# A four-layer cross-attention kernel on one core: the gelu of layer 2 as a tanh of a polynomial, for three batches in four

## What is computed

```
out = attn(layer_norm(q), layer_norm(kv))            # layer 2, 16 heads of 16
out = q + jax.nn.gelu(ctx @ Wo + bo, approximate=False)
...
x = residual + _mha(x, base_n, W_qkv, b_qkv, W_o, b_o)     # layer 3, 8 heads of 32
U = (xn @ W_in.T + b_in) @ Bmat
def step(s, u_t):
    s = jax.nn.silu(s @ A.T) + u_t
    return (s, s)
```

## Time and profile before

| | us |
|---|---|
| median of 3 runs | 1515.5 |
| the runs | 1513.93 to 1517.46 |
| profiled execution, its time | 1517.49 |
| profiled execution, its span | 1515.9 |
| PE busy, share | 1346.9, 89% |
| ACT busy, share | 1065.2, 70% |
| DVE busy, share | 1039.8, 69% |
| POOL busy, share | 82.9, 5% |

### The profile page before, as it was taken

One profiled execution on the slowest core, in us unless ns is written; L12 is line 12 of the kernel. 1 busy time (PEld: TensorE's weight loads), 2 busy tenths in 40 slices (PEclk: granted clock), 3 DMA queues, 4 the chain that ended last, 5 costly groups with the idle time before them and its releaser, 6 DMA issues.

```text
span 1515.9 us, 35932 instructions
## 1 busy us (share of the span) xinstructions
PE 1346.9 (89%) x13436; PEld 1002.6 (66%) x13436; DVE 1039.8 (69%) x2323; ACT 1065.2 (70%) x3212; POOL 82.9 (5%) x145
## 2 busy tenths in 40 slices
PE   7999899988998889999888999988899999788855
PEld 6788666665675556777666677766676777566644
DVE  4676757756787778687777777877776787777400
ACT  4556677757788887777787677777866777787422
POOL 2000111110000000000000000000000000000000
PEclk9999999999999999999999999999999999999855
DMA  8222310012221122121101211201121121110100
GB/s 296 85 87 98 103 56 2 1 46 95 58 85 42 44 75 68 42 71 57 57 30 57 83 31 58 85 29 54 47 70 43 43 85 57 29 50 9 43 0 14
DMA packets 69883, 90.42 MB, mean 60 GB/s; under 512 B 5520, under 2 KB 58896, under 8 KB 69328
## 3 DMA queue, kind: packets, MB, share of 16 engines
q1 hardware_dynamic: 69600, 87.87, 18.2%
q0 software_dynamic: 112, 0.26, 0.1%
HBM read 71.33 MB, written 16.78 MB: 58 GB/s over the span
## 4 chain that ended last, share of the span: by engine, by line
PE 60%; DVE 14%; ACT 14%; issue 10%; POOL 0%; DMA 0%; ACTq 0%; DVEq 0%; SPq 0%; POOLq 0%
PE ps L1320 14%; PE ps L1694 11%; PE ps L1327 8%; PE ps L1334 7%; PE ps L1723 6%; ACT arena L790 5%; DVE arena L1269 5%; PE ps L1768 3%; PE ps L1397 2%; PE ps L1521 2%; PE ps L1538 2%; PE ps L1677 2%; DVE arena L949 2%; ACT R L850 1%; DVE nmax L1252 1%
## 5 line engine op out<-in xcount | busy, mean ns | idle before, releaser
L1320 PE MATMUL ps<-W,arena 128*128 128x128 f32 x2896 | 434.6, 284 | 22.3 <-ACT arena L790 19.8
L1320 PEld LDWEIGHTS ps<-W,arena 128*128 128x128 f32 x2896 | 324.9, 145 | 171.5 <-issue 129.5
L790 ACT ACTIVATE arena<-ps,nmax 128x512 f32<-128x512 f32 x640 | 435.1, 686 | 0.2
L797 ACT COPY arena<-ps 128x512 f32<-128x512 f32 x320 | 187.3, 585 | 213.0 <-PE ps L1320 208.9
L1249 DVE TENSOR_REDUCE nmax<-ps 128x1 f32<-128x512 f32 x320 | 206.1, 686 | 119.5 <-PE ps L1694 83.3
L1269 DVE COPY arena<-ps 128x512 f32<-128x512 f32 x320 | 213.8, 686 | 23.7 <-PE ps L1320 13.5
L1694 PE MATMUL ps<-W,arena 32*128 32x512 f32 x1280 | 185.2, 646 | 35.3 <-DVE arena L1269 34.2
L1723 PE MATMUL ps<-arena 128*32 128x128 f32 x5120 | 173.4, 276 | 31.6 <-ACT arena L797 31.4
L1252 DVE TENSOR_REDUCE nmax<-ps 128x2 f32<-128x1024 f32 x160 | 193.7, 1210 | 0.0
L1723 PEld LDWEIGHTS ps<-arena 128*32 128x32 f32 x5120 | 130.4, 110 | 69.5 <-ACT arena L797 59.1
L790 ACT ACTIVATION_READ_ACCUMULATOR arena<-ps,nmax 128x1 f32 x640 | 131.1, 205 | 0.0
(11 more groups left out here) (240 smaller groups left out, 1648.0 us busy)
## 6 DMA issues: line engine op xcount, KB each, us to landing
W<-keys SPq DMA_DIRECT2D x48, 512.0 KB, 3.7
arena<-values SPq DMA_DIRECT2D x48, 512.0 KB, 5.1
keys<-W SPq DMA_DIRECT2D x16, 448.0 KB, 3.0
values<-W SPq DMA_DIRECT2D x16, 448.0 KB, 3.6
W<-keys SPq DMA_DIRECT2D x16, 256.0 KB, 2.8
arena<-values SPq DMA_DIRECT2D x16, 256.0 KB, 3.3
W<-in_pack SPq DMA_DIRECT2D x1, 3180.0 KB, 10.5
CX<-in_ctx SPq DMA_DIRECT2D x4, 512.0 KB, 11.0
```

What stands on the lines that cost most here:

```text
L790: nc.scalar.activation(Pr[:, a, :], ps[:, a, :], ACT.Exp, bias=nmax[:, u % 32:u % 32 + 1], accum_out=den[:, u % 32:u % 32 + 1]).then_inc(s ...
L797: nc.scalar.copy(PT[:, (4 * Q + a) % 8, :, :].rearrange("p k n -> p (k n)"), psT).then_inc(sem("u_ev_act"), 1)
L1320: ins = nc.tensor.transpose(dst[:, k * P:(k + 1) * P], src[:, k * P:(k + 1) * P], ident)
```

## The change

For the batches 0 to 2 the gelu is computed as 0.5 x (1 + tanh(p(x))). POOL computes p(x): it clamps x to +-5.7, squares it, and evaluates a polynomial of seven coefficients in the square by multiply and add in turn, then multiplies by x. That is 14 instructions of 128 x 256 values in float32, each behind a wait for the one before. ScalarE takes the tanh of the result in place (L793 in the new numbering), and VectorE puts the rest together in two instructions (L1262 and L1264) in place of one add. The new tiles `bent` lie in the part of `W` that held `inw`, which is not used any more by then. The batch 3 keeps its gelu and its steps. In the chains of the batches 0 to 2 gelu, statistics, norm and transpose move four steps back, from 4, 5, 6, 6 to 8, 9, 10, 10, and what hangs on the transpose with them; POOL's part stands at step 3. Calls of `after_steps` get the batch as a second argument.

```diff
@@ -132,11 +134,18 @@
-def after_steps(li):
+ERF_AT = 5.7
+ERF_TANH = (0.7978849414816304, 0.03633308446488688, -3.2594837808075025e-05, -5.5306259012116404e-05,
+            3.964757753935919e-06, -1.322645093331823e-07, 1.7562063102252576e-09)
+ERF_OPS = 2 * len(ERF_TANH)
+def after_steps(li, b):
-                 2: dict(gelu=4, stats=5, nrm=6, tp=6), 3: dict(bias=2, stats=3, nrm=4, tp=4)}[li])
+                 2: dict(gelu=8, stats=9, nrm=10, tp=10) if b < 3 else dict(gelu=4, stats=5, nrm=6, tp=6), 3: dict(bias=2, stats=3, nrm=4, tp=4)}[li])
...
@@ -305,6 +314,8 @@
+        spare = Carve(W[:, PLAN["inw"][0]:PLAN["outw"][0]])
+        bent = [[spare.take(D) for _ in range(3)] for _ in range(2)]
...
@@ -499,12 +510,36 @@
             pool.memset(UT[:, (NCH - 1) * P + 1:NCH * P, NB - 1], 0.0)
             pool.memset(UT[:, 0, :], 0.0).then_inc(sem("zeroed"), 1)
 
+            def bend(c, b):
+
+                x, x2, r = bent[b % 2]
+                n = 3 * c + b
+                done = itertools.count(ERF_OPS * n + 1)
+                if n:
+                    pool.wait_ge(sem("L2_gelu"), c * NB + b + 1 - 1)
+                pool.wait_ge(sem("L2_pre"), c * NB + b + 1)
+                nc.gpsimd.tensor_scalar(x, orows[b % 2], ERF_AT, -ERF_AT, ALU.min, ALU.max).then_inc(sem("L2_bent"), 1)
+                pool.wait_ge(sem("L2_bent"), next(done))
+                nc.gpsimd.tensor_tensor(x2, x, x, ALU.mult).then_inc(sem("L2_bent"), 1)
+                pool.wait_ge(sem("L2_bent"), next(done))
+                nc.gpsimd.tensor_scalar(r, x2, ERF_TANH[-1], ERF_TANH[-2], ALU.mult, ALU.add).then_inc(sem("L2_bent"), 1)
+                for a in ERF_TANH[-3::-1]:
+                    pool.wait_ge(sem("L2_bent"), next(done))
+                    nc.gpsimd.tensor_tensor(r, r, x2, ALU.mult).then_inc(sem("L2_bent"), 1)
+                    pool.wait_ge(sem("L2_bent"), next(done))
+                    nc.gpsimd.tensor_scalar(r, r, a, None, ALU.add).then_inc(sem("L2_bent"), 1)
+                pool.wait_ge(sem("L2_bent"), next(done))
+                nc.gpsimd.tensor_tensor(r, r, x, ALU.mult).then_inc(sem("L2_bent"), 1)
+
             def chain_of(o, b):
                 G, wq = OCTETS[o]
                 c, li, _ = STAGES[G]
                 if LAYERS[li].quads != 2 * (wq + 1):
                     return
-                n, step = turn_side(G), after_steps(li)
+                n, step = turn_side(G), after_steps(li, b)
+                if li == 2 and b < 3:
+                    yield step["add"]
+                    bend(c, b)
                 if li:
                     yield step["stats"]
                     norm({1: "L2", 2: "L3", 3: "u"}[li], n, b % 2)
...
@@ -753,8 +788,12 @@
-                    act.wait_ge(sem("L2_pre"), n)
-                    nc.scalar.activation(nrm[i], orows[i], ACT.Gelu).then_inc(sem("L2_gelu"), 1)
+                    if b < 3:
+                        act.wait_ge(sem("L2_bent"), ERF_OPS * (3 * c + b + 1))
+                        nc.scalar.activation(bent[i][2], bent[i][2], ACT.Tanh).then_inc(sem("L2_gelu"), 1)
+                    else:
+                        act.wait_ge(sem("L2_pre"), n)
+                        nc.scalar.activation(nrm[i], orows[i], ACT.Gelu).then_inc(sem("L2_gelu"), 1)
...
@@ -1218,7 +1257,14 @@
-                    add_more(row, row, nrm[i])
+                    if b < 3:
+                        own["sums"] += 2
+                        nc.vector.scalar_tensor_tensor(orows[i], bent[i][2], 1.0, orows[i], ALU.add, ALU.mult).then_inc(sem("row_sum"), 1)
+                        dve.wait_ge(sem("row_sum"), own["sums"] - 1)
+                        nc.vector.scalar_tensor_tensor(row, orows[i], 0.5, row, ALU.mult, ALU.add).then_inc(sem("row_sum"), 1)
+                        dve.wait_ge(sem("row_sum"), own["sums"])
+                    else:
+                        add_more(row, row, nrm[i])
```

More of the change, by code:

```diff
@@ L741, in chain_of @@
                 c, li, _ = STAGES[G]
-                l, i, n, step = LAYERS[li], b % 2, turn_side(G), after_steps(li)
+                l, i, n, step = LAYERS[li], b % 2, turn_side(G), after_steps(li, b)
                 if l.quads != 2 * (wq + 1):
```

1 line of the change is left out of this document (added).

## The result

| | before | after |
|---|---|---|
| median, us (20 executions each) | 1515.27 | 1519.78 |
| the executions, us | 1511.69 to 1518.57 | 1513.73 to 1527.24 |
| ratio, 95% interval | | 1.0031 [1.0016, 1.0046] |
| profiled execution, its time, us | 1517.49 | 1515.4 |
| its span, us, and granted clock | 1515.9, 0.961 | 1513.8, 0.961 |

The forecast was 1512.3. The median moved the other way, by +4.5 us, while the two profiled executions, which had the same granted clock of TensorE, differ by 2.1 us in the direction of the forecast. That contradiction is what the experiments are about.

The account below looks back on a forecast made before the run. The prediction took a loop run once per quad of four heads, across several engines, as the bound. Chunk 0 +0.6, chunks 1 to 3 -6.2 and the collision +2.4 gave -3.2 us: 1515.5 to 1512.3, range 1496 to 1521.

Parts of the forecast that it names:

- The bounding views: What bounds the kernel: no engine is full; the loop each quad of four heads runs once, TensorE 60% of chain.
- part 1: Third quad of a stage loses two table loads and the gelu: -1.38 us in chunk 0, -2.27 later.
- Part 2: Norm, transpose, query projection and evictions go from a stage's fourth quad (-0.71, -0.86 us) to the next stage's second (+0.93, +1.08).
- Part 3: VectorE's add and statistics, now ahead of the copies in the next stage's first quad, delay the following scores: +1.36 us.
- Part 4: Third batch's query evictions meet the fourth batch's gelu on ScalarE: 0.6 us once per chunk, +2.4 in all.
- Part 5: POOL's polynomial, 7.5 to 10.7 us, is covered by two whole quads and about 2 us more: costs nothing.
- The sum: Chunk 0 +0.6 us, chunks 1 to 3 -6.2, the collision +2.4: together -3.2 us.
- The step from the sum to the median: The -3.2 us summed from the profiled execution is applied to the median of 1515.5, giving 1512.3 us.
- D is worse than its parts: Rival: work queued in the next stage's second quad adds 0.4 us per batch, +4.8, so 1517 us; chance 0.17.

## Why the prediction was wrong

**The bounding views and part 1 (loads and gelu leave A): right.** A is 5.54 in chunk 0 and 5.86 later, forecast 5.55 and 5.86. ScalarE lost 30.1 us, forecast 30.8.

**Part 2 (projection from B to D): right in chunk 0, half in the others.** B is 5.55 in chunk 0, forecast 5.54. In the scan chunks it is 6.05, 5.99 and 5.67 for the three batches, forecast 5.63 for all. I had read one batch's B in before and used it for nine, and that very batch, the second, came out at 5.99: -0.50, forecast -0.86. The tail was misread. In chunk 0 I took it from C, in chunk 1 from 785.99 to 788.18, which is D and has 2.19 us. C's own, in before, starts here and ends at the scores of 782.23, 2.42 us:

```profile
779.81 0.66 PE L1320 MATMUL ps<-W,arena 128*128 128x128 f32 x4
```

In after that B's tail is 2.55:

```profile
773.65 0.65 PE L1366 MATMUL ps<-W,arena 128*128 128x128 f32 x4
...
776.20 1.14 PE L1740 MATMUL ps<-W,arena 32*128 32x512 f32 x8 [0.32 <-DVE arena L1315]
```

D was spared a part of what B kept: it is 6.81, 6.83 and 6.79, and for the second batch +0.88, forecast +1.08 (7.03). In chunk 0 it is 6.55, forecast 6.59.

**Part 3 (VectorE's block in C): right.** +1.38 in chunk 0, forecast +1.36; 7.13 to 7.14 later, forecast 7.22. The releaser of D's scores is L1315, as forecast, and C ahead of it was not free. The run with the block one step later shows the same from the other side: C falls by 1.37.

**Part 4 (the collision): right in kind, the term too small.** Two rows of before in chunk 3, the copy of ScalarE that starts A' and the values that wait for the second one:

```profile
1368.69 0.59 ACT L797 COPY arena<-ps 128x512 f32<-128x512 f32 x1
...
1371.60 1.08 PE L1723 MATMUL ps<-arena 128*32 128x128 f32 x32 [0.61 <-ACT arena L797]
```

and the same place of after:

```profile
1363.32 1.16 PE L1373 MATMUL ps<-arena,W 128*128 128x128 f32 x8
...
1364.95 0.59 ACT L836 COPY arena<-ps 128x512 f32<-128x512 f32 x1 [0.35 <-PE ps L1366]
...
1365.50 0.61 ACT L761 ACTIVATE arena<-ps,bq 128x128 f32<-128x128 f32 x2
...
1368.36 1.08 PE L1769 MATMUL ps<-arena 128*32 128x128 f32 x32 [1.55 <-ACT arena L836]
```

The scores of A' start at 1369.14 in before and at 1364.96 in after. Before, ScalarE's copy was 0.45 us ahead of them, now it is level. Its row says that it waited 0.35 us for a transpose of TensorE. Two things that part 2 moved stand ahead of it in D now, the query projection on TensorE (L1373) and the evictions of the norm on ScalarE (L748); no run separates them there. So from scores to values it is 3.40 in place of 2.46: +0.94. The evictions are 0.5 of it, as two runs show (8.76 against 8.25 where they alone are added, 8.68 against 9.18 where they alone are taken away), a little under the 0.6 that I counted, and 0.4 is the lost lead, which I did not count. Four times 0.94 is +3.7, forecast +2.4.

**Part 5 (POOL): right that it costs nothing, its length too short.** A polynomial took 11.2 us, above the forecast range of 7.5 to 10.7, and still ended 1.8 us before the tanh of 486.03. Its first and last instruction, timeline of POOL:

```profile
473.01 0.40 POOL L521 TENSOR_SCALAR W<-arena 128x256 f32<-128x256 f32 x1 [13.89 <-DVE arena L1257]
...
483.46 0.73 POOL L532 TENSOR_TENSOR W<-W 128x256 f32<-128x256 f32 x1
```

The tensor_scalar in place took 0.853, outside my upper bound of 0.765. That bound rested on the tensor_tensor, "which reads twice as much", being the longer of the two; at 0.728 it was the shorter. The estimate by the Trainium skill ("GPSIMD Engine Reference", section on elementwise cycle accounting), under 0.6, was further off still; the rows of L530 disagree with it, those of L521 and L525 (0.40 us) do not.

**The sum: right, in part by luck.** By the traces' quads at clock 1.00, chunk 0 is +0.17 for each batch (forecast +0.20), the others are -0.77, -0.61 and -1.14 for the three batches (forecast -0.69), and the collision is +3.7: +0.5 - 7.6 + 3.7 = -3.4 us, forecast -3.2. The third batch's larger gain, which I had not read for itself (mostly in its D, +0.71 where I had +1.08), cancels the collision's excess.

**The step from the sum to the median: wrong.** It read "a difference carries over", and so put the clock at nothing. That holds only if both kernels are granted the same clock. Beside each other they got 0.9590 and 0.9636, and after had 0.9578 in the result's own executions. On the line of after a fall from 0.9635 to 0.9578 is 7.7 us, which carries 1512.4 to 1520.1. The clock was in view: the traced execution of before was listed at 0.961 with 1517.5 us, 2 above the median. I noted the 2 us and did not ask what they were. Nor did the rival "D is worse than its parts", whose 1517 lies nearest on the slow side, happen: D was shorter than forecast. No rival had the mechanism. The collision in A' is shown to be a source of the lower clock from both sides: added alone to before it takes 0.0032 (standard error 0.0009), and taken out of the change it gives 0.003 to 0.004 back. The gap in the four C of layer 3, put alone into before, took 0.0016, which six executions against eleven do not tell from noise; as a second source it is likely but not shown. Together that would be 0.0048, near the 0.0046 to 0.0058 of the change. That they simply add is an inference, and against it stands the run with the first two batches, which has long C and a collision in layer 2 and lost no clock (the gelu's waits in two A a chunk are gone there too). A mean clock of four executions is uncertain by some 0.001.

**Open.** Which property of a quad lets the clock fall. Many stretches begin behind waits of TensorE, but most quads with such a wait have none, and the same kernel has them at other places from one execution to the next. Where the lower clock of the slow executions of after fell is not on record either: only two of its 32 were traced, at 0.961 and 0.959, and none at 0.953.

## What to carry to other kernels

A sum of waits taken from one trace predicts the time at an equal clock. Before it is set against a median, ask whether the change adds or removes a wait of TensorE, and expect that it may cost more than its length if it adds one: here 5.9 us of gaps cost 8.8, and 2 us of a collision 5.4, while the long C of the first two batches cost nothing on top. Work moved off one engine's critical slot pays only if it lands in a slot where its new engine would wait: the same block cost 1.4 us ahead of the copies, and 0.4 ahead of the maxima half a quad later. When several steps are moved, look at each place where a moved and an unmoved chain now meet, with the lead that every engine brings to it.

## What the runs showed of the hardware

- The granted clock of TensorE differs between executions of one kernel (after: 0.953 to 0.963, 1527 to 1514 us), and its mean differs between kernels with nearly the same busy times. What a stretch at the 1.2 GHz level costs depends on the quad: 0.2 and 1.0 us in two A of before, nothing in an A of the kernel with gaps in layer 3 (8.13 us with it and without, chunk 2), 1.6 us in a D of after and at a chunk's end in both. The Trainium skill ("TensorE: Matmul & The Clock Gate", section on what is actually happening) puts the penalty of the ramp at under 1% of a typical kernel's span and advises against fitting to a count of slow matmuls. The difference between two kernels here is of that size (7.7 us of 1520 is 0.5%), but a change worth 0.2% is decided by it.
- On POOL a tensor_scalar of 128x256 took 0.40 us with two constants and two tiles (L521, L525), and 0.853 us as an add of one constant in place (L530), longer than the tensor_tensor of the same size, 0.728 (0.613 where it squares one tile, L523). Which of the two differences matters no run here separates.
- POOL's 121 us of polynomial beside a busy VectorE changed no quad. The Trainium skill ("SBUF — State Buffer", section on who interferes with whom) says that POOL and VectorE exclude each other in some forms; in the slots of this kernel nothing of it reached the path.
